# A graph network whose first table is built inside the scan of the adjacency matrix, with x in parts and the weights on ScalarE's queue

## The chip, the core and the metric

The kernel runs on one core of a Trainium2 chip. Its engines are TensorE (PE in the profile, weight loads PEld), VectorE (DVE), ScalarE (ACT), GpSimd (POOL) and SyncE (SP, which only issues transfers); they meet through semaphores. Sixteen DMA engines move data between memory (HBM) and the core. The metric is device time in microseconds (us), less is better.

## The reference

Two graph layers over 8192 nodes with 128 features, each with a residual. The adjacency matrix is 8192 x 8192 in float32, 268 MB, and has about two ones in a row.

```python
h = relu(layernorm(x))
wh = (h @ weight).reshape(n, 4, 32)                  # layer 0: attention with 4 heads
e = leaky_relu(parent[:, None] + child[None, :])     # parent, child: wh against att_weight
x = x + einsum(softmax(where(adj > 0, e, -9e15)), wh)
h = relu(layernorm(x))
msg = relu((adj @ h) @ W_msg.T + b_msg)              # layer 1: sum over neighbours, then a GRU
x = x + gru_cell(msg, h, W_ih, W_hh, b_ih, b_hh)
```

## The kernel before

The 8192 rows are 64 tiles of 128 rows, and four tiles make a row group (NG = 16 groups, index s; in the table's code q). The kernel has three stages.

**Table.** Of h the kernel makes, for each q, `wh` and the attention terms, and stores them in HBM as `wh_table`, from which neighbours' rows are gathered later. The chain for one q: four rows are normed (`relu0` on ScalarE, into `h_buf`), four transposes (`turn0`, TensorE), a copy out of PSUM that also sums (`turned0`, ScalarE), four products with the weights `wx` (`project`, TensorE), three copies (`table`, VectorE), and a store (GpSimd's queue). The store leaves from `t_buf`, which has two buffers, so `table(q)` waits until the store of q-2 has landed (`table_out`). Layer norm's statistics of all 64 tiles (`bn_stats`) come ahead of it, and the weights have to be turned first (`wtr_done`, `wtr_out`).

**Scan.** Each row tile of the matrix is read as two halves of 128 x 4144 and 128 x 4048, some 2 MB each. In this document m = 2 x tile + half numbers them from 0 to 127: load m, indicate m. There are SLOTS = 4 buffers `adj_in`; `indicate` (ScalarE) makes a bf16 indicator of half-tile m, and only then is its slot free for load m + 4 (SyncE waits for `ind_done`). `pack` (TensorE) folds a tile's indicator into words with 60 matmuls, `search` (VectorE) takes the maxima, and then the neighbours' lists, gathers, attention and the message `g_table` follow, one to three groups behind, in an order that the function `schedule` and each engine's `body` write out by hand. A tile's `indicate` waits for the `pack` of two tiles before.

**Second layer.** Gathers of `g_table` rows, gates, and stores of the output.

Before the change SyncE issues x, the weights, the biases and then the first four loads. ScalarE runs indicate 0 and 1, then the whole table stage, and then indicate 2. All engines walk through the table stage as a loop of two q in a step.

## Time and profile before

| | |
|---|---|
| median of 3 runs | 1160.13 us (1158.62 to 1164.36) |
| the profiled execution's own time | 1159.31 us |
| its span, first to last instruction | 1157.6 us |
| busy share PE / DVE / ACT / POOL | 59% / 51% / 59% / 51% |
| moved by DMA | 311.92 MB, 269 GB/s over the span |
| indicate 0 to indicate 127 | 46.3 to 782.8 us |
| second layer's gathers | from 875.5 us |

No engine is busy for more than 59% of the span. Rows show what an engine did and, where it had idled, for how long and what released it. Issue to landing of a transfer is the time from its issue to its last byte and semaphore.

### The profile page before, as it was taken

The numbers are of one execution on the slowest core, as the hardware profiler recorded it, in microseconds if no ns is written. First come the engines' busy times: TensorE is split into PE (matmuls) and PEld (weight loads), VectorE is DVE, ScalarE is ACT, GpSimd is POOL, SyncE is SP. The second block draws the span as 40 slices with busy tenths as digits, with TensorE's granted clock in tenths as the row PEclk, the third lists the DMA queues.
The fourth block names the chain that finished last, engine by engine and source line by source line (L and its number), as shares of the span: only waits on it lengthen the run. The fifth ranks groups of instructions, "written<-read, shape, count | busy, mean of one in ns | idle before, by whom it ended". The sixth has DMA issues, their size and how long they took to land. (4 is left out here: it accounts for less than half of the span.)

```text
span 1157.6 us, 14697 instructions
## 1 busy us (share of the span) xinstructions
PE 679.1 (59%) x4141; PEld 523.0 (45%) x4141; DVE 586.4 (51%) x2487; ACT 686.2 (59%) x723; POOL 592.6 (51%) x598
## 2 busy tenths in 40 slices
PE   0076555765665566566566566655332776777774
PEld 0064334554454454354354444444331565555563
DVE  4632524656656646747647647557331244433443
ACT  0497866886887887788778778772210333233331
POOL 0021074464564654654744744735705777777770
PEclk9997887888788788778878878876555989899998
DMA  7748999999999999999999999951101222222220
GB/s 237 308 149 306 428 401 413 412 411 416 393 396 413 390 413 407 389 406 405 393 413 403 392 413 398 388 224 20 42 5 44 60 67 68 57 68 70 67 66 25
DMA packets 58623, 311.92 MB, mean 269 GB/s; under 512 B 15577, under 2 KB 32994, under 8 KB 42210
## 3 DMA queue, kind: packets, MB, share of 16 engines
q1 hardware_dynamic: 30434, 277.37, 58.8%
q0 software_dynamic: 19712, 30.02, 10.7%
q10 hardware_dynamic: 8448, 4.20, 1.2%
q8 instruction: 12, 0.20, 0.1%
q14 instruction: 17, 0.14, 0.0%
HBM read 298.82 MB, written 12.71 MB: 269 GB/s over the span
## 5 line engine op out<-in xcount | busy, mean ns | idle before, releaser
L457 ACT ACTIVATE ind<-adj_in 128x4144 bf16<-128x4144 int32 (+1 forms) x128 | 461.9, 3609 | 39.1 <-DMA adj_in<-in_adj 22.8
L397 POOL DMA_INDIRECT rows_in<-wh_table,idx x192 | 198.2, 1032 | 304.4 <-DVE val_idx L869 250.7
L602 PE MATMUL ps<-ind,bit_w 128*128 128x296 bf16 (+1 forms) x1792 | 312.2, 340 | 0.0
L602 PEld LDWEIGHTS ps<-ind,bit_w 128*128 128x128 bf16 x1792 | 206.9, 115 | 89.9
L1030 POOL DMA_INDIRECT rows_in<-g_table,idx x192 | 197.6, 1029 | 91.3 <-issue 54.0
L401 POOL DMA_INDIRECT vals_in<-in_adj,val_idx x192 | 183.6, 956 | 58.6 <-issue 58.6
L799 DVE MAX8 cand<-ps 128x8 f32<-128x148 f32 x256 | 61.9, 304 | 117.6 <-PE ps L602 117.2
L598 PE MATMUL ps<-idx_r,idx_w 128*128 128x296 bf16 x128 | 44.2, 346 | 129.8 <-ACT ind L457 129.6
L1164 DVE TENSOR_SCALAR ownT<-iota,edge_row 128x128 f32<-128x128 f32 x64 | 14.7, 324 | 152.6 <-DMA rows_in<-g_table,idx 152.5
L598 PEld LDWEIGHTS ps<-idx_r,idx_w 128*128 128x128 bf16 x128 | 15.8, 123 | 140.4 <-ACT ind L457 126.5
L619 PE MATMUL ps<-rest,tri 128*128 128x4 f32 x32 | 9.0, 352 | 115.0 <-DVE rest L833 115.0
L1266 ACT ACTIVATE adj_in<-ps 128x1024 f32<-128x1024 f32 x16 | 16.4, 1025 | 77.1 <-PE ps L1360 77.1
L619 PEld LDWEIGHTS ps<-rest,tri 128*128 128x128 f32 x32 | 7.6, 296 | 119.3 <-DVE rest L833 119.3
L408 POOL DMA_DIRECT2D wh_table<-t_buf x16 | 12.3, 767 | 83.8 <-DVE t_buf L778 83.2
L1343 PE MATMUL ps<-b_rows,ones_b 96*128 96x128 bf16 x64 | 16.6, 260 | 62.6 <-DVE rows_in L1166 62.6
L1360 PE MATMUL ps<-wT,adj_in 128*128 128x384 f32 x128 | 51.9, 487 | 0.0
L887 DVE TENSOR_SCALAR pen<-mask 128x8 f32<-128x8 f32 x16 | 5.2, 322 | 83.0 <-PE ps L611 83.0
L1258 ACT ACTIVATE adj_in<-ps 128x512 f32<-128x512 f32 x16 | 9.6, 597 | 61.4 <-PE ps L1346 61.4
L1268 ACT ACTIVATE adj_in<-adj_in 128x512 f32<-128x512 f32 x16 | 10.1, 630 | 56.1 <-DVE adj_in L1176 56.1
L494 ACT COPY pm<-pm 128x32 f32<-128x32 f32 x16 | 3.5, 218 | 66.8 <-DVE pm L896 66.8
L624 PE MATMUL ps<-pm,own 128*128 128x8 f32 x128 | 19.4, 278 | 36.6 <-DVE pm L896 36.6
L509 ACT ACTIVATE sd<-mv,epsc 128x4 f32<-128x4 f32 x16 | 4.8, 297 | 59.8 <-DVE mv L936 59.8
(220 smaller groups left out, 1514.7 us busy)
## 6 DMA issues: line engine op xcount, KB each, us to landing
adj_in<-in_adj SPq DMA_DIRECT2D x64, 2072.0 KB, 15.0
adj_in<-in_adj SPq DMA_DIRECT2D x64, 2024.0 KB, 14.0
wh_table<-t_buf POOLq DMA_DIRECT2D x16, 264.0 KB, 3.0
g_table<-t_buf ACTq DMA_DIRECT2D x16, 256.0 KB, 25.1
out<-adj_in SPq DMA_DIRECT2D x16, 256.0 KB, 2.3
rows_in<-wh_table,idx POOLq DMA_INDIRECT x192, 6.7
vals_in<-in_adj,val_idx POOLq DMA_INDIRECT x192, 6.7
rows_in<-g_table,idx POOLq DMA_INDIRECT x192, 2.8
```

What stands on the lines that cost most here:

```text
L397: nc.gpsimd.indirect_dma_start(out=rows_in[:, par, t, k, :], out_offset=None, in_=wh_table, in_offset=bass.IndirectOffsetOnAxis(ap=idx[:, ...
L401: nc.gpsimd.indirect_dma_start(out=vals_in[:, par, t, k:k + 1], out_offset=None, in_=adj_values, in_offset=bass.IndirectOffsetOnAxis(ap=va ...
L457: nc.scalar.activation(ind[:, t % 2, a:b], adj_in[:, slot, 0:b - a].bitcast(I32), ACT.Relu, bias=1.0, scale=-1.0, accum_out=empty[:, bass. ...
L598: nc.tensor.matmul(o, idx_w[:], idx_r[:, u * HALF:(u + 1) * HALF], start=True, stop=False)
L602: ins = nc.tensor.matmul(o[:, 0:w], bit_w[:, b, :], ind[:, t % 2, c0:c0 + w], start=False, stop=(b == BITS - 1))
L619: nc.tensor.matmul(ps_off, tri[:], rest[:], start=True, stop=True).then_inc(off_done, 1)
L624: ins = nc.tensor.matmul(ps_pm[:, t, :], own[:, par, t, :], pm[:, t, :], start=True, stop=True)
L799: ins = V.max(cand[:, t, j * 8:(j + 1) * 8], ps[:, (t % 2) * 2 + j // 2, a:b])
L1030: nc.gpsimd.indirect_dma_start(out=rows_in[:, par, t, k, 0:D], out_offset=None, in_=g_table, in_offset=bass.IndirectOffsetOnAxis(ap=idx2[: ...
L1266: nc.scalar.activation(rzt[:], ps[:, 0:G, 0:2 * D], ACT.Tanh, scale=0.5).then_inc(rz_done, 1)
L1343: nc.tensor.matmul(o, ones_b[:], b_rows[:, 4 * D:5 * D], start=True, stop=False)
L1360: ins = nc.tensor.matmul(o[:, 0:3 * D], msgT[:, t, :], wT[:, 1:4, :].rearrange("p c d -> p (c d)"), start=False, stop=True)
```

## The change

Four things are done.

1. SyncE's queue begins with the four first loads of the matrix; then it takes the biases (own semaphore `b_in`), then the later loads.
2. x is loaded from GpSimd's queue in 8 pieces of 8 tiles, two for each of four parts of XC = 16 tiles (`x_in[c]`). The weights and attention vectors (12 transfers) are issued from ScalarE's queue. TensorE still waits for all 12 (`w_in`) before its first instruction.
3. The table stage is no longer a stage: its steps are woven into `body(0)` and `body(1)`, in the order that `units(m)` gives: q = 2m-4 and 2m-3 for m = 2 to 7, and q = m+4 for m = 8 to 11. The norm's rows move from ScalarE to VectorE (`rows0`, without the relu), and relu is part of `turned0`. `project` has one pair of PSUM banks in place of two, so `project(q)` waits for `table(q-1)`. The statistics are made by parts (`variance0`, `norm0`), the biases' rows at m = 13.
4. `pack` works by halves: the matmuls of a tile's first half wait only for the first indicate.

```diff
+        def units(m):
+            if 2 <= m < 2 * G:
+                return (2 * m - 4, 2 * m - 3)
+            if 2 * G <= m < 3 * G:
+                return (m + G,)
+            return ()
+        def turn_bank(q):
+            return 4 if q % 2 and q < 3 * G else 7
...
             @block.sync
-                sp.dma_start(x1[:], x_rows).then_inc(x_in, 16)
-                sp.dma_start(wx[:, 0:D], weight).then_inc(w_in, 16)
...
                 for n in range(SLOTS):
                     load(n // 2, n % 2, n)
+                sp.wait_ge(const_done, 1)
+                for r in (0, 32, 64):
...
             @block.gpsimd
+                for c in range(T // XC):
+                    for n in range(2):
+                        tt = c * XC + n * (XC // 2)
+                        pool.dma_start(x1[:, tt:tt + XC // 2, :], x_rows[:, tt:tt + XC // 2, :]).then_inc(x_in[c], 16)
...
             @block.scalar
+                act.dma_start(wx[:, 0:D], weight).then_inc(w_in, 16)
+                act.dma_start(w_raw[:, 0, :], W_msg).then_inc(w_in, 16)
+                act.dma_start(w_raw[:, 1:4, :], W_ih.rearrange("(c p) d -> p c d", p=P)).then_inc(w_in, 16)
+                act.dma_start(w_raw[:, 4:7, :], W_hh.rearrange("(c p) d -> p c d", p=P)).then_inc(w_in, 16)
...
-                    nc.scalar.activation(hT[:, par].rearrange("p g d -> p (g d)"), ps[:, (7, 4)[par], :], ACT.Identity,
+                    nc.scalar.activation(hT[:, q % 2].rearrange("p g d -> p (g d)"), ps[:, turn_bank(q), :], ACT.Relu,
...
+                    def scan(t, half):
+                        indicate(s, t, half)
+                        if isinstance(s, int) and s < 2:
+                            m = s * 2 * G + 2 * t + half
+                            if m < T // XC:
+                                deviation0(m)
+                            for q in units(m):
+                                turned0(q)
...
             @block.tensor
+                def project(q):
                     pe.wait_ge(hT_done, q + 1)
+                    if q >= 1:
+                        pe.wait_ge(table_rows, q)
...
                 def pack(s, t):
                     tile = s * G + t
-                    pe.wait_ge(ind_done, tile * 2 + 2)
...
+                    for half in range(2):
+                        pe.wait_ge(ind_done, tile * 2 + half + 1)
...
+                        if isinstance(s, int) and s < 2:
+                            m = tile * 2 + half
+                            for q in units(m):
+                                project(q)
+                            for q in units(m + 1):
+                                turn0(q)
...
             @block.vector
+                def rows0(q):
+                    if q >= 2:
+                        dve.wait_ge(htr_done, q - 1)
+                    for t in range(G):
+                        n = q * G + t
+                        ins = V.tensor_scalar(h_buf[q % 2][:, t, :], x1[:, n, :], rs0[:, n:n + 1], nmr0[:, n:n + 1], ALU.mult, ALU.add)
+                    ins.then_inc(h_done, 1)
...
+                def woven(m):
+                    for q in units(m):
+                        table(q)
+                    for q in units(m + 1):
+                        if q >= 2:
+                            rows0(q)
...
                 def body(s, par, do):
+                    early = isinstance(s, int) and s < 2
...
+                    if early:
+                        woven(s * 2 * G)
+                        woven(s * 2 * G + 1)
                     if "c" in do:
                         search(s, 0)
```

What this does to ScalarE's order at the program's start. Before, after the square root of the deviations (L426) and the first two indicates (L457), rows of q (L433) and `turned0` (L441) follow one another:

```order
L426 ACTIVATE sd<-var,epsc 128x64 [waits var_done]
L457 ACTIVATE ind,empty<-adj_in 128x4144 [waits adj_in0]
L457 ACTIVATE ind,empty<-adj_in 128x4048 [waits adj_in1]
L433 ACTIVATE rows_in<-x,nmr,rs 128x128 [waits ln0_done]
L433 ACTIVATE rows_in<-x,nmr,rs 128x128 x3
```

After it, an indicate (L461), a square root (L444) and two `turned0` (L451) take turns:

```order
L461 ACTIVATE ind,empty<-adj_in 128x4144 [waits adj_in0]
L444 ACT_TABLE_LOAD
L444 ACTIVATE sd<-var,epsc 128x16 [waits var_done]
L461 ACTIVATE ind,empty<-adj_in 128x4048 [waits adj_in1]
L444 ACTIVATE sd<-var,epsc 128x16 [waits var_done]
L461 ACTIVATE ind,empty<-adj_in 128x4144 [waits adj_in2]
L444 ACTIVATE sd<-var,epsc 128x16 [waits var_done]
L451 ACTIVATE hT,hsum<-ps 128x512 [waits htr_done] x2
L461 ACTIVATE ind,empty<-adj_in 128x4048 [waits adj_in3]
```

Indicate 1, 2 and 3 each stand behind a square root of one part of x, and indicate 3 also behind `turned0`.

VectorE after the change, from the first norm to the third part's statistics (wxT, wT, wx are the turned weights; h and attn hold the rows of even and odd q):

```order
L763 RECIPROCAL rs<-sd 128x16 [waits sd_done]
L764 SCALAR_TENSOR_TENSOR nmr<-mean,rs 128x16 [waits dve_step]
L795 COPY wxT<-ps 128x128 [waits wtr_done,dve_step]
L797 COPY wT<-ps 128x512 [waits wtr_done]
L798 COPY wT<-ps 128x384
L800 COPY wx<-ps 128x8 [waits wtr_done]
L772 TENSOR_SCALAR h<-x,rs,nmr 128x128 x4
L772 TENSOR_SCALAR attn<-x,rs,nmr 128x128 x4
L751 BN_STATS st<-x 128x6 [waits x_in2]
```

The statistics of the third part stand behind the copies of the turned weights.

TensorE after the change, at m = 3 and into m = 4 (L592 pack, L570 `project`, L562 `turn0`):

```order
L592 MATMUL ps<-ind,bit_w 128x296 [waits ind_done]
L592 MATMUL ps<-ind,bit_w 128x296 x12
L592 MATMUL ps<-ind,bit_w 128x200
L570 MATMUL ps<-wx,hT 128x136 [waits table_rows,hT_done]
L570 MATMUL ps<-wx,hT 128x136 x3
L570 MATMUL ps<-wx,hT 128x136 [waits table_rows,hT_done]
L570 MATMUL ps<-wx,hT 128x136 x3
L562 MATMUL ps<-ident,h 128x128 [waits hT_done,h_done]
L562 MATMUL ps<-ident,h 128x128 x3
L562 MATMUL ps<-ident,attn 128x128 [waits hT_done,h_done]
L562 MATMUL ps<-ident,attn 128x128 x3
L588 MATMUL ps<-idx_r,idx_w 128x296 [waits seg_done,ind_done]
```

A half-tile's matmuls, two projections and the next pair's transposes now follow one another.

## Rows read from the trace of the kernel before

**Rows 1.** Stretches: length; PE, PEld, DVE, ACT, POOL busy; granted clock; DMA share; GB/s.

```profile
27.00:42.00 15.00, 0.00 (x0) 0.00 (x0) 13.91 (x57) 0.00 (x0) 0.00 (x0) 1.00 1.00 429
44.00:120.00 76.00, 47.91 (x304) 38.22 (x305) 21.80 (x77) 65.64 (x114) 12.27 (x16) 0.91 0.62 232
120.00:740.00 620.00, 376.52 (x2461) 282.37 (x2459) 363.01 (x1759) 488.81 (x400) 322.07 (x325) 0.80 1.01 405
```

**Rows 2.** Timeline of ScalarE: start, us; indicates 0, 2, 4, 16, last.

```profile
46.30 3.64 ACT L457 ACTIVATE ind<-adj_in 128x4144 bf16<-128x4144 int32 x1
...
88.48 3.65 ACT L457 ACTIVATE ind<-adj_in 128x4144 bf16<-128x4144 int32 x1
...
103.16 3.66 ACT L457 ACTIVATE ind<-adj_in 128x4144 bf16<-128x4144 int32 x1 [7.38 <-PE ps L602]
...
156.06 3.66 ACT L457 ACTIVATE ind<-adj_in 128x4144 bf16<-128x4144 int32 x1 [2.27 <-DMA adj_in<-in_adj]
...
779.31 3.58 ACT L457 ACTIVATE ind<-adj_in 128x4048 bf16<-128x4048 int32 x1
```

**Rows 3.** Timeline of SyncE's queue: the first matrix loads.

```profile
22.52 31.58 SPq L378 DMA_DIRECT2D adj_in<-in_adj  x6
```

**Rows 4.** Landing of load 4, issued at 50.3 us into an empty queue.

```profile
DMA to landing us min/median/max: 7.4/7.4/7.4
```

**Rows 5.** DMA summary of 0 to 120 us: packet sizes, x.

```profile
DMA packets 6320, 30.78 MB, mean 256 GB/s; under 512 B 889, under 2 KB 1922, under 8 KB 4994
...
x<-in_x SPq DMA_DIRECT2D x1, 0.5 KB, 17.5
```

**Rows 6.** The page's DMA queues: ScalarE's, packets and MB.

```profile
q10 hardware_dynamic: 8448, 4.20, 1.2%
```

**Rows 7.** Landing of g_table stores issued 235 to 724 us.

```profile
DMA to landing us min/median/max: 24.2/25.7/26.6
```

**Rows 8.** Landing of g_table stores issued 810 to 872 us.

```profile
DMA to landing us min/median/max: 2.3/2.3/2.3
```

**Rows 9.** DMA summary of 60 to 90 us: GpSimd's queue, wh_table stores.

```profile
q0 software_dynamic: 960, 3.24, 35.0%
...
wh_table<-t_buf POOLq DMA_DIRECT2D x12, 264.0 KB, 2.9
```

**Rows 10.** Landing of the last wh_table store, issued at 97.0 us.

```profile
DMA to landing us min/median/max: 10.2/10.2/10.2
```

**Rows 11.** Timeline of the start: weights turned, statistics of 16 tiles.

```profile
23.79 1.70 PE L551 MATMUL ps<-ident,ownT 128*128 128x128 f32 x7
...
28.47 3.80 DVE L748 BATCH_NORM_STATS2 st<-x  x16 [0.36 <-DVE b_rows L743]
```

**Rows 12.** Timeline of the table stage: transposes, projection, copies.

```profile
71.60 0.60 PE L562 MATMUL ps<-ident,rows_in 128*128 128x128 f32 x4
...
72.18 1.17 PE L570 MATMUL ps<-wx,hT 128*128 128x136 f32 x8
...
74.17 0.17 DVE L776 COPY parent<-ps 128x16 f32 x1 [2.13 <-DMA wh_table<-t_buf]
...
74.37 0.70 DVE L778 COPY t_buf<-ps 128x528 f32<-128x528 f32 x1
```

**Rows 13.** Timeline of TensorE: the same 14 pack matmuls twice, and a later gap.

```profile
97.63 3.65 PE L602 MATMUL ps<-ind,bit_w 128*128 128x296 bf16 x14
...
101.24 1.89 PE L602 MATMUL ps<-ind,bit_w 128*128 128x296 bf16 x14
...
783.03 0.43 PE L598 MATMUL ps<-idx_r,idx_w 128*128 128x296 bf16 x1 [3.92 <-ACT ind L457]
```

**Rows 14.** Timeline of VectorE: four tensor_scalar of 128x128.

```profile
144.39 0.86 DVE L871 TENSOR_SCALAR ownT<-iota,recv 128x128 f32<-128x128 f32 x4
```

**Rows 15.** Busy time by stretch: VectorE in decode and in list_neighbours.

```profile
122.70:126.90 4.20, 1.98 (x9) 1.27 (x10) 3.81 (x19) 4.20 (x3) 0.00 (x0) 0.78 1.03 435
131.50:134.80 3.30, 0.00 (x0) 0.00 (x0) 3.15 (x22) 2.02 (x2) 0.00 (x0) 1.00 0.99 422
```

More of the change, by code:

```diff
@@ L42 @@
 NEI0 = (127 + IBITS) * WORDS
-W_DMAS = 4 + 2 * H + 9
+W_DMAS = 4 + 2 * H
+B_DMAS = 9
+XC = 16
 TW = D + H
@@ L233, in gat_gru_kernel @@
         ps_tr = ps[:, 7, :].rearrange("p (g d) -> p g d", g=G)
-        x_in = sem("x_in")
+        x_in = [sem(f"x_in{i}") for i in range(T // XC)]
+        b_in = sem("b_in")
         w_in = sem("w_in")
@@ L523, in body @@
                     if "c" in do:
-                        indicate(s, 2, 0)
+                        scan(2, 0)
                     if "g" in do:
@@ L529, in body @@
                     if "c" in do:
-                        indicate(s, 2, 1)
+                        scan(2, 1)
                     if "g" in do:
@@ L533, in body @@
                     if "c" in do:
-                        indicate(s, 3, 0)
+                        scan(3, 0)
                     if "b" in do:
@@ L537, in body @@
                     if "c" in do:
-                        indicate(s, 3, 1)
+                        scan(3, 1)
                     if "b" in do:
@@ L604, in pack @@
-                    ins.then_inc(pack_done, 1)
+                    for half in range(2):
+                        pe.wait_ge(ind_done, tile * 2 + half + 1)
+                        if half == 0 and (not isinstance(tile, int) or tile >= 2):
+                            pe.wait_ge(seg_done, tile - 1)
+                        for u in range(2):
+                            o = ps[:, (t % 2) * 2 + u, 0:HALF]
+                            if half == 0:
+                                nc.tensor.matmul(o, idx_w[:], idx_r[:, u * HALF:(u + 1) * HALF], start=True, stop=False)
+                            for b in range(half * (BITS // 2), (half + 1) * (BITS // 2)):
+                                c0 = b * WORDS + u * HALF
+                                w = min(HALF, N - c0)
+                                ins = nc.tensor.matmul(o[:, 0:w], bit_w[:, b, :], ind[:, t % 2, c0:c0 + w],
+                                                       start=False, stop=(b == BITS - 1))
+                        if half:
+                            ins.then_inc(pack_done, 1)
+                        if isinstance(s, int) and s < 2:
[4 more added lines that the diff above has]
+                                turn0(q)
+                            if m == 3 * G:
+                                mean_row()
@@ new lines, in columns_of, with variance0 @@
+                def columns_of(a, c):
+                    return a[:, c * XC:(c + 1) * XC]
+                def variance0(c):
+                    dve.wait_ge(x_in[c], 32)
+                    for t in range(c * XC, (c + 1) * XC):
+                        ins = V.bn_stats(st0[:, t, :], x1[:, t, :])
+                    link(ins)
+                    st = st0[:, c * XC:(c + 1) * XC, :]
+                    mean, half, var = columns_of(mean0, c), columns_of(half0, c), columns_of(var0, c)
+                    V.tensor_tensor(half, st[:, :, 1], st[:, :, 4], ALU.subtract)
+                    V.tensor_tensor(mean, st[:, :, 1], st[:, :, 4], ALU.add)
+                    link(V.tensor_tensor(var, st[:, :, 2], st[:, :, 5], ALU.add))
+                    link(V.scalar_tensor_tensor(out=half, in0=half, scalar=0.25, in1=half, op0=ALU.mult, op1=ALU.mult))
+                    V.scalar_tensor_tensor(out=var, in0=var, scalar=1.0 / D, in1=half, op0=ALU.mult, op1=ALU.add).then_inc(var_done, 1)
@@ L970, in body @@
                         search(s, 2)
+                    if early:
+                        woven(s * 2 * G + 6)
+                        woven(s * 2 * G + 7)
                     if "b" in do:
```

214 lines of the change are left out of this document (84 added, 130 removed).

## The prediction

> **What bounds the kernel now.** I read the page first: no engine is busy for more than 59% of the span. So I took the busy time by stretch, with the DMA engines' share. From 120 to 740 us that share is 1.01 at 405 GB/s [rows 1]: in the scan the DMA engines are the bound, and TensorE, VectorE and ScalarE have slack (377, 363 and 489 of 620 us). From 44 to 120 us the share is only 0.62 [rows 1], which is 76 x 0.38 = 29 us in which nothing moved. ScalarE's timeline says why: indicate 0 starts at 46.3 us, indicate 1 right behind it, indicate 2 only at 88.5 [rows 2], since the table stage stands between them, and until then two of the four slots stay full and no load can be issued. SyncE's queue says what comes ahead: the first load is issued at 22.5 us [rows 3], behind x and the weights. From load 16 on the scan is paced by landings: indicate 16 starts at 156.06 us after 2.27 us of waiting for its load [rows 2]. That is the mark of my sum. If load 16 lands d us later, everything up to the last load is d us later, because the same bytes follow at the same full share. Then comes a tail, in which indicate 127 starts at 779.3 us [rows 2] for another reason than its load (below).
>
> **Where the weights land.** The change puts three queues beside each other from the start: the matrix on SyncE's, x on GpSimd's, the weights on ScalarE's. Rows show how a queue fares beside the matrix. A `g_table` store from ScalarE's queue lands in 2.3 us when nothing else runs [rows 8] and in 25.7 us beside the matrix [rows 7]. The page counts 8448 packets for 16 such stores [rows 6], 528 each: one for each of 512 rows of 512 B and one that closes the transfer on each of 16 engines, so 33 to an engine. (25.7 - 2.3) / 33 = 0.71 us for a packet. A matrix row of 16.4 KB at 429 GB/s / 16 [rows 1] takes 0.61 us. So the engines seem to serve the queues in turn, packet by packet, and a small packet pays for a large one. The weights' packets are small too: between 512 B and 2 KB there are 1922 - 889 = 1033 in the first 120 us [rows 5], and the weights have 128 + 128 + 384 + 384 = 1024 rows of 512 B. To an engine that is 64 packets, 16 for the attention vectors' single values and 12 closing ones: 92 turns. GpSimd's stores are 960 packets for 12 [rows 9], 5 to an engine, so 8 rows to a packet; x in 8 pieces of 1024 rows is 8 x (8 + 1) = 72 turns, each of 4 KB or some 0.23 us, since x alone took 17.5 us [rows 5], 2 of them overhead.
>
> A turn of all three is thus 0.61 + 0.23 + 0.03 = 0.87 us, and a load (8 packets and a closing one) takes 8 x 0.87 + 0.26 = 7.2 us. From 2 us on loads 0 to 3 land at about 10.5, 18, 25 and 32. Indicate 0 ends at 14 and frees load 4. Indicate 1 stands behind the first square root, which needs x part 0: 18 turns, 18.5 us, then 16 statistics at 3.8 us [rows 11] and a few small operations, 23.6. It ends at 28 (load 5). Indicate 2 needs part 1: 36 turns, 33 us, plus 5, and ends at 42 (load 6). The matrix queue therefore never runs dry, and seven loads pass until 54 us in 63 turns; the weights have had 63 of 92, and the other 29, with the last of x, take 3 us more. They land at 57; if an x packet costs two matrix packets, as the last `wh_table` store's 10.2 us [rows 10] suggests, the matrix runs dry for some us and they land at 50 to 53. I take 55 (bounds 50 and 60).
>
> A rule of the Trainium skill weighs against this. Its page "DMA: Bandwidth & Descriptors", section "Queues, rings and completion order", says that each engine goes round the queues by packet, and that a packet holds 9 to 17 descriptors typically. This trace agrees on the turns (0.71 us beside 0.61) and not on the size, for these transfers: one row to a packet on the hardware queues. By the rule's packets the weights would need under 30 turns and land near 25 us, and the sum would be that of the first rival below.
>
> **The table stage, woven.** TensorE does nothing before the weights are there, `wx` needs the turned copies (eight transposes, of which seven take 1.70 us [rows 11], two copies, one product: 3.5 us), and VectorE holds parts 2 and 3 of the statistics behind them. From W (weights landed), VectorE: +3.5 copies; 8 rows, 1.8 (four such operations take 0.86 [rows 14]); part 2, 5.0; a norm, 0.6; part 3, 5.0; two norms, 1.1; search, 1.0: table(0) starts at W + 18.3. At m = 2 follow table(0), projection (1.17), table(1), rows of q = 2 and 3, their transposes (0.60 [rows 12]): 0.9 + 1.3 + 0.9 + 1.8 + 0.7, so W + 24. Table is 0.9: from 74.17 to 75.07 [rows 12]. ScalarE can start indicate 4 then.
>
> From there each m with two q is one chain, since `project` now waits for the table before it and the rows for both: transposes 0.65, pack of a half 1.9 (14 matmuls [rows 13]), 2 x 1.17, 2 x 0.9, 2 x 0.9 and some 0.5 of handing over, **9.0 us, where a load takes 4.9** alone (2.1 MB at 429 GB/s [rows 1]). Four such steps (m = 4 to 7, the last with one row set less) take 36: W + 60. For m = 8 to 11 one q each costs about 6 us, plus decode (4.2) and list_neighbours (3.3) [rows 15] and two searches on VectorE, in total 31: indicate 12 starts at W + 91, 3.8 us later load 16 is issued, and lands 7.4 us after [rows 4]. With W = 57 that is 159.4. The matrix queue idles through m = 3 to 11, as it did before.
>
> Corrections. W = 55: -2. TensorE's granted clock: the same 14 matmuls take 3.65 us at half the clock (1.2 GHz) and 1.89 at full (2.4 GHz), and the long one follows a gap of several us [rows 13]; here the wait for table(0) and three places in m = 8 to 11 leave such gaps: 0 to +9, I take +5. The stores: table(q+2) needs store(q), 0.8 us after its table and 2.9 to land in the clear [rows 9], 10.2 beside the matrix [rows 10]; a chain of 9.0 covers up to 7.3 us of landing; I take +2. Load 16 lands at 159.4 - 2 + 5 + 2 = 164.4, **8.4 us later than before**.
>
> **What costs nothing or gives.** The norm's rows on VectorE and the smaller ScalarE work are in the chain above. One more activation-table load lies before the first square root, which waits for x anyway. The biases land behind load 3, needed at m = 13. Gathers wait for all 16 stores; these are out before m = 13, as the first gather needs. Packing by halves gives nothing while DMA is the bound. In the tail it gives: indicate 127 waits for a chain that begins with the pack of tile 62, and the last pack begins only after it (783.0, 3.92 us of gap [rows 13]). Each of these packs, 3.65 + 1.89 or more, is halved behind its last indicate: 2 us and 2.5 us, from which I take 0.5 because VectorE is then still weighing. **-4** (bounds 0 and -5). Sum: +8.4 - 4 = +4.4 on 1159.3, the profiled execution's own; it stood 0.8 below the median, so **1164.5 us**.
>
> **The rivals.**
> - *The weights are not held up*, because an engine takes several of their rows in a turn. Speaks for it: the turn's price was measured on stores, and the weights are loads. Against it: the 1033 small packets [rows 5]. VectorE reaches the copies at 38.5 us; with the weights there by then it goes on 16.5 us sooner than with W = 55: 1148. (By the rule of the Trainium skill named above, this is what would happen.)
> - *Full cover.* If moreover x comes quickly and the chain hides in load time, the idle 29 us [rows 1] goes, with the tail's 4: 1127. Against it: 9.0 us per step beside 4.9.
> - *Slower by the stores.* If store(q) lands in 10.2 us in every step, as beside the matrix at 97 us [rows 10], the step is 0.9 + 0.8 + 10.2 = 11.9 us in place of 9.0: four times 2.9 is +12 where I took 2, 1175. It decides from 7.3 us of landing on. Against it: the matrix queue idles for nearly half of each step.
>
> **How the numbers follow.** My forecast 0.60 (own range 1154 to 1174; in it 0.05 faster, 0.35 no change, 0.20 slower), weights not held up 0.20, full cover 0.08, stores 0.12. No change is within 0.5% (5.8 us, about what a measurement of this kernel can tell). Faster 0.33, same 0.35, slower 0.32. The range leaves out full cover and the upper part of the stores' case: 1141 to 1176.
>
> **What would show it.** In the profile after: landings of the first four loads about 7 us apart; TensorE's first instruction near 55 us (under 40: the first rival); indicate 2 near 38 and indicate 3 near 68; indicates 4 to 8 some 9 us apart, ended by TensorE's transposes, with VectorE's copies waiting for TensorE (in the stores' case for the store, over 2 us each); DMA share under 0.7 between 60 and 150; indicate 16 starting near 164; from there to the last load the same time as before; the last indicate to the second layer's first gather shorter by some 2 us. I am wrong if weights or x land much earlier than turns by packet allow, or if a step takes well under 9 us.

## The result, and the profile after

The changed kernel takes 1183.91 us (median of 4 runs, 1182.01 to 1190.3), before it on the same chip 1159.75 (4 runs, 1158.62 to 1164.36). The ratio is 1.021, with a 95% interval of 1.0162 to 1.0259: the change costs 2%. The forecast was 1164.5 in a range that ended at 1176. The profiled execution took 1182.82 us in place of 1159.31, and its span is 1181.1 us against 1157.6: 23.5 us to find.

I laid the starts of all 128 indicates beside those of before, and so split the 23.5 us by place. The matrix is read in this order whatever else happens, so the difference at indicate m is what the kernel has lost by then. First the timeline of ScalarE in the changed kernel, with indicates 2, 3, 4, 8, 12, 13, 14, 16 and 127, and two operations between them (start, duration, and in brackets idle time and its releaser):

```profile
40.25 3.64 ACT L461 ACTIVATE ind<-adj_in 128x4144 bf16<-128x4144 int32 x1
...
64.84 0.31 ACT L444 ACTIVATE sd<-var,epsc 128x16 f32<-128x16 f32 x1 [20.86 <-DVE var L759]
...
66.92 3.58 ACT L461 ACTIVATE ind<-adj_in 128x4048 bf16<-128x4048 int32 x1
...
79.50 3.65 ACT L461 ACTIVATE ind<-adj_in 128x4144 bf16<-128x4144 int32 x1
...
120.66 3.65 ACT L461 ACTIVATE ind<-adj_in 128x4144 bf16<-128x4144 int32 x1
...
154.23 3.65 ACT L461 ACTIVATE ind<-adj_in 128x4144 bf16<-128x4144 int32 x1
...
163.36 0.21 ACT L493 COPY recv<-ps 128x64 f32<-128x64 f32 x1 [5.39 <-PE ps L629]
163.47 3.58 ACT L461 ACTIVATE ind<-adj_in 128x4048 bf16<-128x4048 int32 x1
167.04 3.65 ACT L461 ACTIVATE ind<-adj_in 128x4144 bf16<-128x4144 int32 x1
...
174.24 3.65 ACT L461 ACTIVATE ind<-adj_in 128x4144 bf16<-128x4144 int32 x1
...
802.78 3.58 ACT L461 ACTIVATE ind<-adj_in 128x4048 bf16<-128x4048 int32 x1
```

Against [rows 2] indicate 0 starts 27 us earlier, indicate 4 23.7 earlier, indicate 16 18.2 later (174.24 - 156.06), indicate 20 15.9 later, indicate 124 28.4 later, indicate 127 23.5 later (802.78 - 779.31). The second layer's first gather is 21.0 later (896.47 against 875.51), the end 23.5. So the start loses 16, the middle (indicates 20 to 124) 12, the end of the scan gives 7 back, and the second layer loses 2.5. The sum forecast was +8, 0, -4, 0. The 12 of the middle are a difference of two: at indicate 48 the kernel is only 9.9 us behind (348.27 against 338.42), and it loses 18.5 from there to indicate 124.

Busy time by stretch shows where the matrix queue idles (columns as in [rows 1]: the last three are granted clock, DMA share, GB/s):

```profile
27.00:42.00 15.00, 0.00 (x0) 0.00 (x0) 4.25 (x23) 4.26 (x4) 0.00 (x0) 1.00 1.00 380
55.00:70.00 15.00, 12.39 (x72) 9.48 (x72) 12.00 (x58) 4.54 (x6) 0.00 (x0) 1.00 0.00 0
80.00:120.00 40.00, 26.38 (x153) 19.99 (x152) 16.92 (x64) 18.80 (x22) 6.02 (x8) 0.84 0.71 245
120.00:160.00 40.00, 24.46 (x141) 17.87 (x138) 19.25 (x90) 21.46 (x20) 4.42 (x6) 0.80 0.78 271
160.00:200.00 40.00, 25.38 (x155) 17.64 (x156) 23.32 (x112) 29.45 (x18) 21.99 (x24) 0.83 0.92 359
```

Until the weights are there the DMA engines are full (1.00). Then nothing moves for 15 us, and the share stays under 0.8 until 160 us. In before the queue was full again from 120 us on [rows 1]. The hole has moved, and grown: the scan now starts early, but it stops at indicate 2, waits for the weights, and then goes at the table's pace.

The timeline of the start and of one step (m = 5, queues and all engines) shows both:

```profile
13.58 4.34 ACTq L440 DMA_DIRECT2D a_blk<-in_L_gnn_att_weight  x1
...
35.98 3.19 DVE L751 BATCH_NORM_STATS2 st<-x 128x6 f32<-128x128 f32 x16 [10.58 <-DMA x<-in_x]
...
55.62 0.45 PE L549 MATMUL ps<-ident,wx 128*128 128x128 f32 x1 [55.62 <-DMA a_blk<-in_L_gnn_att_weight]
...
89.67 3.57 ACT L461 ACTIVATE ind<-adj_in 128x4048 bf16<-128x4048 int32 x1
...
91.05 1.19 PE L592 MATMUL ps<-ind,bit_w 128*128 128x296 bf16 x7
92.08 1.09 PE L570 MATMUL ps<-wx,hT 128*128 128x136 f32 x8
...
93.20 0.17 DVE L780 COPY parent<-ps 128x16 f32<-128x16 f32 x1 [4.45 <-PE ps L570]
...
95.42 0.17 DVE L780 COPY parent<-ps 128x16 f32<-128x16 f32 x1 [1.35 <-PE ps L570]
...
96.21 1.11 DVE L772 TENSOR_SCALAR h<-x,rs,nmr 128x128 f32<-128x128 f32 x4
...
97.23 1.11 DVE L772 TENSOR_SCALAR attn<-x,rs,nmr 128x128 f32<-128x128 f32 x4
97.37 0.66 PE L562 MATMUL ps<-ident,h 128*128 128x128 f32 x4 [1.99 <-DVE h L772]
...
98.40 1.11 PE L562 MATMUL ps<-ident,attn 128*128 128x128 f32 x4 [0.36 <-DVE attn L772]
...
100.13 3.65 ACT L461 ACTIVATE ind<-adj_in 128x4144 bf16<-128x4144 int32 x1
```

TensorE's first instruction waits 55.62 us for the last attention vector. The step is the single chain that the prediction described: pack, projections, tables, rows, transposes. It takes 10.3 us from one indicate to the next.

### The profile page after: what moved, and what is told of

Its sections match the earlier page's. It is cut to its first block and busy times, and to the rows that moved or that the text cites. A ratio compares the mean times of both kernels' runs of the same rounds, so it can differ in the third digit from the quotient of the medians.

```text
span 1181.1 us, 14416 instructions
## 1 busy us (share of the span) xinstructions
PE 723.0 (61%) x4141; PEld 546.4 (46%) x4141; DVE 599.6 (51%) x2571; ACT 666.2 (56%) x663; POOL 599.0 (51%) x606
## 3 DMA queue, kind: packets, MB, share of 16 engines
q0 software_dynamic: 20864, 34.22, 11.2%
## 5 line engine op out<-in xcount | busy, mean ns | idle before, releaser
L461 ACT ACTIVATE ind<-adj_in 128x4144 bf16<-128x4144 int32 (+1 forms) x128 | 462.6, 3614 | 99.6 <-DMA adj_in<-in_adj 95.8
L592 PE MATMUL ps<-ind,bit_w 128*128 128x296 bf16 (+1 forms) x1792 | 336.5, 351 | 47.3 <-ACT ind L461 47.3
L404 POOL DMA_INDIRECT rows_in<-wh_table,idx x192 | 191.7, 998 | 266.0 <-DVE val_idx L897 212.3
L592 PEld LDWEIGHTS ps<-ind,bit_w 128*128 128x128 bf16 x1792 | 208.6, 118 | 157.1 <-ACT ind L461 63.6
L408 POOL DMA_INDIRECT vals_in<-in_adj,val_idx x192 | 187.2, 975 | 58.5 <-issue 58.5
L636 PE MATMUL ps<-rows_in,ident 128*128 128x132 f32 x128 | 32.3, 341 | 35.0 <-DVE rows_in L941 35.0
L588 PE MATMUL ps<-idx_r,idx_w 128*128 128x296 bf16 x128 | 48.3, 377 | 7.1 <-ACT ind L461 5.9
L623 PE MATMUL ps<-pm,own 128*128 128x8 f32 x128 | 24.3, 318 | 42.3 <-DVE pm L924 42.3
L623 PEld LDWEIGHTS ps<-pm,own 128*128 128x128 f32 x128 | 22.8, 267 | 44.7 <-DVE pm L924 44.7
L636 PEld LDWEIGHTS ps<-rows_in,ident 128*128 128x128 f32 x128 | 24.4, 236 | 39.2 <-DVE rows_in L941 39.2
L652 PE MATMUL ps<-wT,hT 128*128 128x128 f32 x128 | 26.3, 369 | 24.6 <-ACT hT L474 24.6
## 6 DMA issues: line engine op xcount, KB each, us to landing
adj_in<-in_adj SPq DMA_DIRECT2D x64, 2024.0 KB, 18.2
```

The costliest lines, as they stand in the source:

```text
L404: nc.gpsimd.indirect_dma_start(out=rows_in[:, par, t, k, :], out_offset=None, in_=wh_table, in_offset=bass.IndirectOffsetOnAxis(ap=idx[:, ...
L408: nc.gpsimd.indirect_dma_start(out=vals_in[:, par, t, k:k + 1], out_offset=None, in_=adj_values, in_offset=bass.IndirectOffsetOnAxis(ap=va ...
L461: nc.scalar.activation(ind[:, t % 2, a:b], adj_in[:, slot, 0:b - a].bitcast(I32), ACT.Relu, bias=1.0, scale=-1.0, accum_out=empty[:, bass. ...
L588: nc.tensor.matmul(o, idx_w[:], idx_r[:, u * HALF:(u + 1) * HALF], start=True, stop=False)
L592: ins = nc.tensor.matmul(o[:, 0:w], bit_w[:, b, :], ind[:, t % 2, c0:c0 + w], start=False, stop=(b == BITS - 1))
L623: ins = nc.tensor.matmul(ps_pm[:, t, :], own[:, par, t, :], pm[:, t, :], start=True, stop=True)
```

## The experiments

All ran on other chips than the first pair (four of them), and on each of these before itself takes 1443 to 1458 us, not 1160. In their traces the start is nearly the same: in the changed kernel, run again, indicates 0 to 18 start within 2.4 us of the first chip's. How far a start can be read is shown by the four later runs whose start is the changed kernel's (two of it, two with whole packs from the third group on): indicate 8 at 120.79 to 121.48 us, indicate 16 at 173.46 to 177.55. A difference of 2 or 3 us at indicate 16 is within that spread. From 200 us on there are stops that the first chip lacks: idle time of TensorE before a pack with no releaser. The granted clock of the loop is lower there too: from 240 to 740 us it is 0.72 to 0.74 in the changed kernel's first repeat, and 0.79 to 0.81 on the first chip. So what follows reads each experiment's **start** as valid for both, and compares **whole times** only on those chips, with the ratio to before on the same chip. Runs of the same kernel agree: the changed kernel is at 0.9789 (0.9763 to 0.9816) and 0.9833 (0.9809 to 0.9858) of before there. It is faster there and slower on the first chip, so the sign of this change depends on the chip, or on something that differed with it; no run came back to the first chip.

> The changed kernel once more, unchanged. The first four experiments ran on a chip on which the kernel before itself took 1458 us in place of 1160, with stops of up to 20 us in the scan of TensorE that the first chip does not show, while indicates 0 to 18 started within 1 us of those on the first chip. So the first 180 us can be read there, the rest not. Here the changed kernel stands beside the kernel before and the kernels below on one chip. On a chip like the first: 1184 beside 1160. On one like the second: unknown; the start as in the first profile in both.

> The changed kernel once more, as the ground of the other three. On a chip on which before takes about 1450 us: 0.979 of before; on one on which before takes 1160 us: 1.021 of it, with the loop at 382 to 397 GB/s and the 17th indicate at 174.3 us on either.

Their indicate 16 starts at 174.29 and 173.46 us.

**1. Weights first.** The 12 transfers of weights and attention vectors leave SyncE's queue ahead of the first loads, in place of ScalarE's queue.

```diff
             @block.sync
+                sp.dma_start(wx[:, 0:D], weight).then_inc(w_in, 16)
...
+                sp.wait_ge(const_done, 1)
+                for h in range(H):
...
                 for n in range(SLOTS):
                     load(n // 2, n % 2, n)
...
             @block.scalar
-                act.dma_start(wx[:, 0:D], weight).then_inc(w_in, 16)
...
```

> The changed kernel with the 12 transfers of weights and attention vectors issued from SyncE, ahead of the matrix's loads; x stays on GpSimd's queue. Theory A (a small packet pays for a large one, weights landed at 55.6 us for that reason): beside x alone the 92 turns cost at most 0.26 us each, so the weights land by 25 us, and TensorE's first instruction is then. Loads start some 20 us later, indicate 0 near 27, indicate 3 near 42 in place of 66.9, and all that follows some 24 us earlier than in the changed kernel, if the woven steps keep their 10.3 us: about 1160. Theory B (the weights were late because 12 transfers on one queue take that long anyway): they land near 50 again and the time is 1184 or more.

Measured: 0.9621 of before (0.9575 to 0.9668), 1403.97 us. The timeline, TensorE's first instruction and indicate 3:

```profile
15.79 0.45 PE L548 MATMUL ps<-ident,wx 128*128 128x128 f32 x1 [15.79 <-DMA a_blk<-in_L_gnn_att_weight]
...
41.21 3.58 ACT L460 ACTIVATE ind<-adj_in 128x4048 bf16<-128x4048 int32 x1 [0.26 <-DMA adj_in<-in_adj]
```

The weights are there 40 us sooner, and indicate 3 starts 25.7 us sooner and waits for its load now. Indicate 16 starts at 148.70, 25.5 us sooner than in the changed kernel and 7.4 sooner than in before. So the place behind the matrix's loads set W, and W sets the start that follows. That it is the turns, packet by packet, rests on the sum of the prediction (92 turns, 55 us), since this run moved the weights to another queue as well as ahead. The steps keep their 10 us each (54.61, 65.22, 75.53, 85.53 for indicates 4 to 7).

**2. Statistics first.** The third and fourth parts' statistics stand ahead of the copies of the turned weights, in VectorE's idle time.

```diff
                 variance0(1)
                 norm0(0)
+                variance0(2)
+                norm0(1)
+                variance0(3)
...
-                variance0(2)
-                norm0(1)
-                variance0(3)
                 norm0(2)
-                norm0(3)
...
```

> The changed kernel with the statistics of parts 2 and 3 of x ahead of the copies of the turned weights on VectorE, and the last norm behind the rows of m = 3. In my prediction 10 us of statistics stood between the landed weights and table(0). Theory A (as predicted, VectorE's statistics are on the path): table(0) starts 10 us sooner, 62 us in place of 72.4, and the kernel gains about 10 us, 1174. Theory B (TensorE's two half packs, transposes and projection, and the indicates, take nearly as long): table(0) waits for the first projection, which ended at 69.1 us, so 3 us are gained: 1181.

Measured: 0.9759 of before (0.9713 to 0.9805), which the changed kernel's 0.9789 and 0.9833 there don't clearly differ from. Indicate 8 starts at 118.76, 2.0 to 2.7 us sooner than in the changed kernel's repeats, although 10 us of work had been moved out of the chain, and at indicate 16 (174.81) nothing is left. The table's first copy comes at 70.38 in place of 72.42: VectorE now waits for x (3.33 us, until 53.84) and then 2.74 us for TensorE's projection. Theory B of the expectation holds.

**3. The step's order.** `table` and `rows0` of two q in turn: table(a), rows(a+2), table(b), rows(b+2), so that TensorE's first transposes need not wait for the second table.

```diff
-                    for q in units(m):
-                        table(q)
-                    for q in units(m + 1):
-                        if q >= 2:
+                    done, ahead = units(m), [q for q in units(m + 1) if q >= 2]
+                    for n in range(2):
+                        for q in done[n:n + 1]:
+                            table(q)
+                        for q in ahead[n:n + 1]:
                             rows0(q)
```

> The changed kernel with VectorE's order within a step turned from table(a), table(b), rows(a+2), rows(b+2) to table(a), rows(a+2), table(b), rows(b+2). Theory A (the step of 10.3 us is one chain through VectorE and TensorE, in which VectorE waits 1.35 us for the second projection and TensorE 2.0 us for rows): the rows fill the first wait and the step becomes about 1.2 us shorter, 9.1 us; over m = 3 to 7 indicate 8 starts 5 to 6 us earlier (115 in place of 120.7), and the whole kernel gains 5 us. Theory B (the step is set by the stores' landings or by the matrix's loads): the step stays at 10.3 us.

Measured: 0.9755 of before (0.9732 to 0.9778). Indicate 8 at 117.76, 3.7 us sooner of 5.7 expected, indicate 9 5.6 sooner, but indicate 12 only 1.0 sooner (154.61 against 155.62) and 13 0.7 later. What the steps give, m = 8 to 12 take back. There TensorE waits for VectorE's rows, 9.3 us in two waits between 120 and 156 us; that these are late because decode and the searches stand ahead of them was not tried by itself.

**4. The wait for `recv`.** `received(0)` goes behind indicate 13.

```diff
+                    late = isinstance(s, int) and s == 1
-                    if "t" in do:
+                    if "t" in do and not late:
                         received(s - 1)
                     if "c" in do:
                         scan(2, 1)
+                    if late:
+                        received(s - 1)
```

> The changed kernel with ScalarE's copy `received(0)` in body(1) moved behind the next indicate, m = 13. In the changed kernel indicate 13 started at 163.5 us after 5.4 us of waiting for that copy's matmuls, which my prediction had not seen. Theory A (the wait stops a load and costs its full length): indicate 13 starts at 158 us, indicates 14 to 16 each 5 us earlier, and the kernel gains 4 to 5 us. Theory B (the next wait takes its place, since VectorE's edge_indices(0) then comes later and tile 7's pack with it): indicate 13 comes earlier but indicates 16 to 20 do not.

Measured: 0.974 of before (0.9708 to 0.9772). From indicate 12 to indicate 13 it takes 3.64 us in place of 7.90, so the wait was real; but indicate 12 starts 1.6 us later, and at indicate 13 the net gain is 2.6 against the changed kernel on the same chip, no more than the spread of such starts.

**5. All four together.**

> The changed kernel with the four edits that shortened its start put together: weights issued ahead of the adjacency loads, statistics of the third and fourth x part ahead of the weights' copies, table and rows of two q in turn on VectorE, and received(0) behind the 14th indicate. If the start is set by the sum of these (weights 24.5 us, the wait for received 2.6, the other two 2.4 and about 1 at the 13th indicate), the 17th indicate starts at 174.3 - 30 = 144 us, 12 earlier than before's 156.1, and the whole is 30 us below the changed kernel on the same chip. If with the weights early something else is late next (the adjacency loads, which the stores and the ten more transfers delay), less than 25 is gained and the 17th indicate waits for its load at 148 or later.

Measured: 0.9616 of before (0.9596 to 0.9636), no better than the weights alone, and its start is worse: indicate 3 at 54.37 against 41.21, indicate 16 at 158.03 against 148.70. VectorE's timeline names the cause, a wait that moved. With the weights early, the fourth part of x lands last, and the copies of the weights stand behind its statistics:

```profile
40.88 3.19 DVE L753 BATCH_NORM_STATS2 st<-x 128x6 f32<-128x128 f32 x16 [7.96 <-DMA x<-in_x]
...
44.82 0.28 DVE L800 COPY wxT<-ps 128x128 f32<-128x128 f32 x1
...
48.20 0.25 DVE L765 RECIPROCAL rs<-sd 128x16 f32<-128x16 f32 x1
```

An order that helped a little while the weights were last hurts when x is last. The last kernel of experiment 7 bears this out: it has the weights and `recv` moved but not VectorE's two orders, and its indicate 3 is at 41.46 again.

**6. Packing by halves, alone and undone.** Before with halves (twice again later), and the changed kernel with whole packs from the third group on (once again).

```diff
-                    pe.wait_ge(ind_done, tile * 2 + 2)
...
+                    for half in range(2):
+                        pe.wait_ge(ind_done, tile * 2 + half + 1)
...
```

> The kernel before with one part of the change: pack by halves, nothing else. In the changed kernel the scan between indicate 20 and indicate 124 took 12 us longer than before, with the DMA share at 1.00 but 382 to 397 GB/s where before had 401 to 405. Theory A (packing by halves frees ScalarE sooner, more loads stand in the queue, and the transfers become slower): this kernel is slower in the same stretch by about 12 us, less some 5 us in the tail: +5 to +8 us in all, 1165 to 1168. Theory B (the rate has nothing to do with it): the scan is as before, and the tail gives 4 to 7 us: 1153 to 1156.

> The kernel before with packing by halves alone, once more, on the chip of the others in this call. Theory A (packing by halves slows the scan's transfers): on a chip like the first 1165 to 1168. Theory B (it does not, and shortens the tail by 4 to 7 us): 1153 to 1156. On the second chip it was 0.942 of before.

> Before with packing by halves alone. On a chip on which before takes about 1450 us: 6% faster, as twice measured. On one on which before takes 1160 us, theory A of the middle (packing by halves makes the loop's transfers slower at a full DMA share) expects 385 to 397 GB/s in 240 to 740 us and a time 8 to 12 us above before; theory B (the rate has nothing to do with the halves) expects 401 to 405 GB/s there, and a time 0 to 5 us below before by the tail.

> The changed kernel, with tiles of group 2 and later packed whole again, so the start is untouched. Theory A: the stretch from indicate 20 to 124 becomes 12 us shorter and the tail 5 to 7 longer: 1177 to 1180. Theory B: the stretch stays as long as in the changed kernel, the tail becomes longer: 1187 to 1191. In both indicate 20 starts near 194 us as in the changed kernel.

> The changed kernel with whole packs from the third row group on. On a chip on which before takes about 1450 us: 1.6% above before, as once measured. On one on which before takes 1160 us, theory A expects the loop's rate back at 401 to 405 GB/s and a time of 1184 - 12 + 7 (the tail's gain lost) = 1179; theory B expects 382 to 397 GB/s to stay and 1184 + 7 = 1191.

Measured: halves alone 0.9422 (0.9382 to 0.9462), 0.9393 (0.9361 to 0.9425) and 0.9414 (0.9367 to 0.946), the last one 1358.82 us; whole packs in the changed kernel 1.0162 (1.0123 to 1.02) and 1.0154 (1.0125 to 1.0183). On these chips the halves are worth 4 to 6%, and all the rest of the change costs 4% (1416 against 1360). In halves alone the start is that of before (indicate 16 at 155.45), so 19 of the 56 us (4% of 1416) are the start. The other 37 or so are in the scan's loop: from indicate 16 to indicate 124 the changed kernel takes 783.0 us where halves alone take 738.9, and on the next chip 773.6 against 743.1. On the first chip this question stays open, as no run came to it again.

**7. The loop's code.** The page's DMA queues hold a line that I had passed over, the instruction packets. In before, and in halves alone too, it is:

```profile
q14 instruction: 17, 0.14, 0.0%
```

The page of the changed kernel has:

```profile
q14 instruction: 43, 0.35, 0.1%
```

Between 240 and 740 us the changed kernel moves 27 of these on the first chip, before 3, so five in each turn of the loop (two row groups). Once in a turn, VectorE stops with no releaser where before it waits 4.28 us for ScalarE. The timeline of VectorE in the changed kernel on the first chip:

```profile
350.79 0.21 DVE L938 TENSOR_TENSOR rows_in<-ex,mask 128x48 f32<-128x48 f32 x1 [6.68 <-issue]
394.24 0.21 DVE L938 TENSOR_TENSOR rows_in<-ex,mask 128x48 f32<-128x48 f32 x1 [4.21 <-ACT ex L497]
...
485.67 0.21 DVE L938 TENSOR_TENSOR rows_in<-ex,mask 128x48 f32<-128x48 f32 x1 [4.34 <-ACT ex L497]
533.10 0.21 DVE L938 TENSOR_TENSOR rows_in<-ex,mask 128x48 f32<-128x48 f32 x1 [6.05 <-issue]
```

VectorE's program is longer ahead of the loop (by 133 instructions in the compiled program, where my count had been 123), and the loop's own, some 300, are the same. To test whether the place of the code does it, memsets of an unused tile were put into VectorE's idle start:

```diff
...
+                for n in range(32):
+                    V.memset(spare[:, n:n + 1], 0.0)
...
```

> Before, with whole packs, and 32 such memsets ahead of its wait for the weights. Theory C with pieces of 64: q14 rises from 17 to about 40 packets, and the time by 20 to 40 us where before takes 1450, by about 10 where it takes 1160. With pieces of 128, or by theory D: 17 packets and no change.

> Before with packing by halves and 32 VectorE memsets in the idle start. q14 goes from 17 to about 42 packets by the place of the code. Theory C (the loading costs): on a chip where before takes 1450 us, 1359 + 38 = 1397 (0.96 of before); where it takes 1160, about 10 us above before. Theory D (it costs nothing): 0.94 of before, as without the memsets.

> The changed kernel with 16 VectorE memsets of a spare tile in the idle start (about 1 us of idle time), so that the loop's code stands 16 instructions later. Theory C (place of the code): q14 falls from 43 to about 20 packets, VectorE's stop once a turn goes, a turn of the loop on a chip where before takes 1450 us falls from 116 to 110 us, and the time from 0.98 to 0.955 of before (38 us less); where before takes 1160 us, about 10 us less. Theory D: 43 packets and the time stay.

> The same with 40 memsets. Theory C with pieces of 64 instructions: the loop of 294 rows again lies across one piece too many, 43 packets and the changed kernel's time (0.98 of before). Theory C with pieces of 128: as with 16, about 20 packets and 0.955. Theory D: as the changed kernel.

> The changed kernel with 5 memsets, which put its loop 128 instructions behind the place it has in before: q14 falls from 43 to about 20 if pieces of 64 or 128 instructions decide, and VectorE's stop once a turn goes. Theory C: 1416 - 38 = 1378 (0.95) where before takes 1450, 10 us less than 1.02 of before where it takes 1160. Theory D: the changed kernel's 0.98 and 1.02. If q14 stays at 43, another distance decides.

> The changed kernel with weights issued ahead of the adjacency loads, received(0) behind the 14th indicate, and the 16 memsets. If the gains add (e3 took 24.5 us off the start, e7 2.6; theory C adds 38 where before takes 1450): 1416 - 13 (what e3 gained in the whole) - 3 - 38 = 1362 there, level with before packed by halves; where before takes 1160, 1184 - 24 - 3 - 10 = 1147. If theory C is wrong, 1400 and 1157.

Measured: with 32 memsets before goes from 17 to 42 packets, and its time stays (0.9985, 0.996 to 1.0011). With the same 32, before with halves also has 42, and goes from 1359 to 1394.78 us, 0.9605 of before (0.9578 to 0.9632), where 1397 was expected. The page of this kernel, and VectorE's timeline:

```profile
q14 instruction: 42, 0.34, 0.1%
```

```profile
374.73 0.21 DVE L916 TENSOR_TENSOR rows_in<-ex,mask 128x48 f32<-128x48 f32 x1 [5.73 <-issue]
435.03 0.21 DVE L916 TENSOR_TENSOR rows_in<-ex,mask 128x48 f32<-128x48 f32 x1 [4.29 <-ACT ex L506]
492.34 0.21 DVE L916 TENSOR_TENSOR rows_in<-ex,mask 128x48 f32<-128x48 f32 x1 [6.14 <-issue]
```

That is the changed kernel's pattern, made by memsets of an unused column. The mark of it is the length of the stop: on these chips halves alone, too, stop there with no releaser named, but for 4.28 us each time. ScalarE's copy of `recv`, once in a row group, comes every 57.97 us (475.09 to 764.95, five groups). With halves alone it came every 54.9 (467.74 to 797.12, six) and, in the first of the three runs, on another chip, every 55.8 (476.88 to 755.82, five); in the changed kernel every 57.65. By the times the price is 1394.78 - 1358.82 = 36 us; by the ratios, which leave the chips' own difference out, (0.9605 - 0.941) x 1450 = 28 (17 to 39 by the ends of the intervals). No chip had both kernels. So **in before with halves the place of VectorE's loop code costs some 28 to 36 us**, about what the changed kernel's loop loses there (37). That it is the same cost in the changed kernel is likely, not shown by taking it away. From indicate m to indicate m + 8, one row group, halves alone (second run) take 54.6 to 54.9 us each time from m = 40 on. In the changed kernel on the same chip 55 and 61 take turns: 54.8, 60.6, 55.1, 60.4, 55.4, 60.9 from m = 40 on. With the 32 memsets it is 56.6, 61.8, 55.4, 61.2, 55.3 (and later 61.2 once more). The extra time comes once in a turn, as the loading does. In before with whole packs it costs nothing, and VectorE's stop there is 4.1 to 4.3 us, no longer than the 4.28 of before on the first chip. That TensorE's longer stops at the pack cover it there (up to 13.0 us, last section) would fit, but was not tried by itself.

The changed kernel with 5, 16 and 40 memsets keeps 43, 43 and 44 packets and its time (0.9809, 0.98, 0.978), so these shifts do not bring the loop back. They don't decide the size of the pieces either: by the compiled program the loop then stands 138, 149 and 173 instructions behind its place in before, none of them a multiple of 64, though the first was meant to be 128. The last kernel (weights first, `recv` later, 16 memsets) has 43 too, so its 0.9577 of before (0.9514 to 0.964; 1390.66 us, where 1362 was expected if the code came back and 1400 if not) is only the start's gain; indicate 16 starts at 147.79. No kernel with the woven table beats before with halves on these chips.

## Why the prediction was wrong, point by point

- **Where the weights land: right.** 55 was taken, TensorE started at 55.62, and the first loads landed 7 us apart as forecast (9.3, 16.1 and 23.1 us). Experiment 1 shows that the weights are late because they stand beside the matrix's loads. The first rival (weights not held up) fell with it. ScalarE's queue held its engine until 17.9 us (the issue at 13.58 takes 4.34) and indicate 0 began at 19.25, not 10.5, at no cost: indicate 2 still waited for x. The prediction set a rule of the Trainium skill against this (page "DMA: Bandwidth & Descriptors", section "Queues, rings and completion order": packets of 9 to 17 descriptors typically), by which the weights would have landed near 25 us. The trace does not agree with it for these rows of 512 B: they landed at 55.62.
- **From W to the steps: right.** table(0) came at W + 16.8 (72.42) against 18.3 (whose terms add up to 18.0), indicate 3 at 66.92 against 68, and the matrix queue idled as the prediction said.
- **The steps: right, once the correction is counted.** "9.0 us, where a load takes 4.9" was 10.3 (indicates 5 to 8 at 89.67, 100.13, 110.23, 120.66), and four times 1.3 is the +5 taken for the clock. The granted clock was 0.84 in 80 to 120 us. In the rows of m = 5 the second transposes take 1.11 (0.60 in [rows 12]), half a pack 3.1 (1.93 and 1.19) in place of 1.9, after idle time of TensorE: these run at 1.2 GHz (the granted clock is 0.50 from 89.1 to 91.05 us and from 98.4 to 99.5), as [rows 13] had one stretch do. Indicate 12, forecast with both corrections at 55 + 91 + 5 + 2 = 153, started at 154.23. Part of that is luck. The 2 us taken for the stores were not needed: one copy waited for a store, 5.63 us, at 124.5, where its neighbours waited 4.4 to 5.0 for TensorE. But the 31 us for m = 8 to 11 were too few: their own terms, 4 x 6 + 4.2 + 3.3 and two searches, make over 31.5, and indicates 8 to 12 took 33.6. (57 + 91 + 3.8 + 7.4 is 159.2, too, and not 159.4.)
- **Behind indicate 12: the step that failed for the start.** The prediction said: "indicate 12 starts at W + 91, 3.8 us later load 16 is issued, and lands 7.4 us after", and made that landing its mark. Load 16 was issued at 158.2 and landed 8.0 us later, at 166.2, not far from the 164.4 of the sum; but it no longer sets anything. ScalarE has `received(0)` between indicates 12 and 13, which waits 5.39 us for TensorE (in before it waits 2.27 us in the same place), and then indicates 13, 14 and 15, each 3.6 us long, ahead of indicate 16. So indicate 16 starts 20.0 us after indicate 12, not 11.2, and loads 17 and on are issued by those late indicates. At indicate 20, where the waits for loads are back, the kernel is 15.9 us behind before, 7.5 more than forecast: 1.2 from indicate 12 and some 6 from this. Experiment 4 shows that the wait is real, and that 2.6 us at most were had by moving it.
- **"in the scan the DMA engines are the bound", "from load 16 on the scan is paced by landings", and so "from there to the last load the same time as before": the second step that failed, by 12 us.** The prediction read the bound from a DMA share of 1.01. ScalarE's waits for the matrix's loads from 330 to 730 us (total, times, longest; us), before and then after, say otherwise:

```profile
ACT ind L457 <- DMA adj_in<-in_adj: 3.4, 6, 1.4
```

```profile
ACT ind L461 <- DMA adj_in<-in_adj: 73.4, 56, 3.5
```

  In before ScalarE hardly ever waited for a load in the loop: each row group (8 indicates) took 44.4 us from indicate 48 on, and what ScalarE waited for was VectorE (`pm` 31.3 us, `sd` 17.7 us). The landings that paced indicate 16 did not pace the loop. The changed kernel took 41.5, 42.8 and 40.6 us for the three groups of indicates 24 to 48, though the DMA share had been full in before. From indicate 48 on it took 45.5 to 46.7, waiting for loads that landed 19.1 us after their issue (median of 450 to 720 us; 15.5 in before). The DMA share from 200 to 740 us is 1.00, but the bytes come slower. Busy time by stretch of before, and then of the changed kernel:

```profile
240.00:450.00 210.00, 127.45 (x848) 96.69 (x847) 129.77 (x618) 167.52 (x142) 115.64 (x116) 0.80 1.01 403
450.00:740.00 290.00, 177.28 (x1189) 134.81 (x1188) 173.56 (x830) 232.47 (x197) 155.78 (x157) 0.81 1.01 403
```

```profile
240.00:450.00 210.00, 144.28 (x894) 106.86 (x892) 127.80 (x614) 169.34 (x143) 116.88 (x120) 0.81 1.01 413
450.00:740.00 290.00, 193.16 (x1124) 141.24 (x1124) 169.91 (x829) 223.78 (x187) 148.30 (x150) 0.79 1.00 385
```

  413 GB/s and then 385, against 403 throughout. Over 500 us that is 198.4 MB in place of 201.5, 3.1 MB or 7.7 us. Why the rate falls stays open. More loads in the queue at once, by the halves, is one candidate (theory A of the first experiment); it was never tested on this chip. The code that is loaded again each turn is another: VectorE's stop is 5.86 to 6.68 us in place of 4.28, some 2 us in each of five turns from 350 us on, and such loading costs 28 to 36 us in before with halves on the other chips. Against it speak that ScalarE waits for loads here and not for VectorE, that the same stops occur at 350 us, where the rate is above before's, and that both groups of a turn are slow here, where on the other chips one of them is.
- **The tail: right in sign.** -7 against -4, between indicate 124 and the first gather; its share between the last indicate and the gather was 2.5 us, where some 2 had been named. The second layer's 2.5 us were in no term.
- **What costs nothing: partly wrong.** "Packing by halves gives nothing while DMA is the bound" needs that bound, which before did not have: on the other chips, where the DMA share from 200 to 400 us is 0.84 to 0.86 with halves, they give 6%.

## What to carry to other kernels

When a long stage is woven into another, price the chain that is left in each step by the slow clock, and then walk the receiving engine's queue to the end of the stretch: an old wait that stood harmless, and the work queued behind it, end last once their slack is gone. A full DMA share does not show that the loads are the bound; look at whether the engine that takes them waits for them. Small transfers beside large ones paid about one large packet for each of theirs here (0.71 us beside 0.61), so weights go first, on the queue that the large loads use; and each such move has to be checked against what then lands last. Compare instruction packets before and after: the same loading at every turn cost nothing in before with whole packs and 28 to 36 us in before with halves.

## What the runs showed of the hardware that I had not expected

- Where a loop's code stands decides whether it stays loaded: 32 VectorE instructions ahead of a loop of some 300 took the instruction packets from 17 to 42.
- The same kernel takes 1160 us on one chip and 1443 to 1458 on four others, with starts alike to 2.4 us, and a change that is 2.1% slower on the first is 1.7 to 2.1% faster on the others. There TensorE stops with no releaser at the packs, and its granted clock is lower: 0.72 from 240 to 740 us in before with 32 memsets, against 0.80 to 0.81 in before on the first chip. The waits of TensorE from 325 to 900 us in before with 32 memsets, and in before with halves (total, times, longest; us):

```profile
PE ps L599 <- issue: 97.3, 9, 13.0
```

```profile
PE ps L604 <- issue: 129.1, 138, 3.1
```

  Nine stops of up to 13.0 us in the one, 138 of up to 3.1 in the other. What TensorE waits for there was not tested, and neither was whether the lower clock is a cause of the longer time or goes with it.
